# Ranks of the second sort: the last 392 columns of edges ranked in layer 0 instead of beside the sorting network

## The reference, cut to what matters

```python
x = _layernorm(x + L0(x, edges))             # mean of x[src] by dst, two matmuls, rows normalized
x = _layernorm(x + L1(x, weight, types))     # relation matrices, (x @ W_r)[src] * w summed by dst
x = _layernorm(x + L2(x, edges))             # 5 rounds: m = h @ W; agg = segment_sum(m[src], dst); GRU
x = _layernorm(x + L3(x, edges, edge_attr))  # edge MLP on x[src], x[dst], attr, summed by src
```

## Time and profile before

| | us |
|---|---|
| median of 3 runs | 9063.8 (9062.63 to 9071.94) |
| profiled execution, its own time | 9073.26 |
| its span, first to last instruction | 9071.5 |
| POOL busy | 6524.4 (72%) |
| PE busy | 6295.3 (69%) |
| DVE busy | 5542.8 (61%) |
| ACT busy | 2574.8 (28%) |

### The profile page before, as it was taken

The page is one execution under the profiler, slowest core; times in us unless marked ns, Lnnn a source line. Parts: engine busy times, 40 slices in busy tenths (PEclk is TensorE's granted clock), DMA queues, the critical chain, the costliest instruction groups (busy, mean ns, idle before and its releaser), DMA issues. The chain is left out here.

```text
span 9071.5 us, 161491 instructions
## 1 busy us (share of the span) xinstructions
PE 6295.3 (69%) x36545; PEld 5409.3 (60%) x36546; DVE 5542.8 (61%) x13908; ACT 2574.8 (28%) x6581; POOL 6524.4 (72%) x7005
## 2 busy tenths in 40 slices
PE   0011255552444498888888888888888999889998
PEld 0000133332333377777777677767776888778887
DVE  9999444442444466656665566656664666556666
ACT  4223111112333211121112111111112333456665
POOL 1777777777777777767777677767776777657776
PEclk9755566665555599999999999999999999989999
DMA  4000222222222244434443444444443444212223
GB/s 153 7 7 18 58 79 77 78 68 61 59 59 59 80 143 137 138 103 143 137 138 108 137 139 136 129 117 138 138 138 104 135 124 127 71 53 63 64 64 53
DMA packets 428100, 870.71 MB, mean 96 GB/s; under 512 B 117433, under 2 KB 229680, under 8 KB 427349
## 3 DMA queue, kind: packets, MB, share of 16 engines
q0 software_dynamic: 269952, 615.62, 25.2%
q10 hardware_dynamic: 122250, 189.76, 6.2%
q1 hardware_dynamic: 35529, 61.49, 2.1%
HBM read 763.02 MB, written 103.40 MB: 96 GB/s over the span
## 5 line engine op out<-in xcount | busy, mean ns | idle before, releaser
L1027 POOL DMA_INDIRECT rows<-state_table,rec x3440 | 3290.6, 957 | 1185.9 <-issue 1105.8
L1100 PE MATMUL l_prod<-rows,onehot 128*125 x10728 | 2640.3, 399 | 1210.6 <-SPq L1041 523.8
L1141 DVE TENSOR_TENSOR agg<-agg,l_prod 125x256 f32 (+2 forms) x5364 | 2038.7, 380 | 2185.2 <-PE l_prod L1100 1156.2
L1100 PEld LDWEIGHTS l_prod<-rows,onehot 128*125 128x125 f32 x10728 | 2010.8, 223 | 1637.4 <-issue 1440.4
L2313 POOL DMA_INDIRECT w_area<-xcol_table,l_slots x832 | 787.7, 947 | 346.6 <-issue 250.4
L1027 POOL DMA_INDIRECT rows<-rel_table,rec x782 | 740.4, 947 | 255.5 <-issue 238.2
L1027 POOL DMA_INDIRECT rows<-in_x_dram,rec x782 | 740.8, 947 | 251.2 <-issue 232.0
L1837 PE MATMUL l_prod<-l_sources,rec 125*125 125x256 f32 x3000 | 695.1, 382 | 24.6 <-DMA rec<-dense_table 23.9
L474 POOL DMA_INDIRECT slots_table<-rec_stage,row_stage x528 | 553.1, 1048 | 161.6 <-issue 143.2
L1837 PEld LDWEIGHTS l_prod<-l_sources,rec 125*125 125x125 f32 x3000 | 562.9, 189 | 118.2 <-DMA rec<-dense_table 30.8
L1792 PE MATMUL l_rh<-state,w_area 128*128 x4000 | 591.0, 282 | 3.0 <-DVE l_u L2121 3.0
(11 more groups left out here) (427 smaller groups left out, 10314.1 us busy)
## 6 DMA issues: line engine op xcount, KB each, us to landing
rec<-dense_table ACTq DMA_DIRECT2D x125, 732.4 KB
rows<-state_table,rec POOLq DMA_INDIRECT x3440
l_sources<-state_table ACTq DMA_DIRECT2D x125, 250.0 KB
rel_table<-l_relrow ACTq DMA_DIRECT2D x50, 500.0 KB
state_table<-l_row ACTq DMA_DIRECT2D x200, 125.0 KB
dense_table<-late_rec SPq DMA_DIRECT2D x50, 366.2 KB
w_area<-xcol_table,l_slots POOLq DMA_INDIRECT x832
rows<-in_x_dram,rec POOLq DMA_INDIRECT x782, 2.5
```

The lines of the kernel that those rows point to most:

```text
L1027: pool.indirect_dma_start(out=K["rows"][:, r, 0:width], out_offset=None, in_=table, in_offset=bass.IndirectOffsetOnAxis(ap=K["rec"][:, wor ...
L1100: last = pe.matmul(slots[k][0:LANES, 0:width], K["onehot"][:, h % ONEHOTS, k, :], rows[:, bass.ds(at[k], width)], start=True, stop=True)
L1141: dve.tensor_tensor(into, into, of, ALU.add).then_inc(S.added, 1)
```

## The change

Of the 784 columns now 392 are late (four of the eight parts), and so POOL scatters 392 in the sort and not 528. Only the first four parts (40 rank turns) are ranked in the sort. POOL keeps the tile numbers, the spare rows and the running bases of the other four in SBUF (`late_bucket`, `late_row`, `late_base`). DVE makes their 40 rank turns in layer 0: five behind every second gather turn, eight times, from turn 4 on; the hardware loop of turns 3 to 24 becomes eight loops of two turns and one of six. All operands of these rank turns lie in SBUF (the numbers compared with, the scan's result and the copies' data too). Their row addresses go to a DRAM table of their own, and a late load is two DMAs. ACT packs the late records in two passes of 196 columns, at turns 16 and 18 of the network. Late columns: 16 in layer 1, 63 in each of rounds 0 to 3, and 124 behind the last round's gathers, in two batches of 62; the second is loaded after SP's relay of the last round and after the first batch has landed.

```diff
-LATE_PIECES = 7
+LATE_PIECES, LATE_PASSES = 6, 2
-LATE = 256
-LATE_LAYER0, LATE_LAYER1, LATE_ROUND, LATE_LAST = 0, 10, 46, 62
+LATE = 392
+LATE_LAYER1, LATE_ROUND, LATE_LAST = 16, 63, 62
+RANK_TILES = 5
+RANK_TURNS = TILES // RANK_TILES
@@ sort_edges, SP
-            sp.wait_ge(late_made, LATE_PIECES)
-            sp.dma_start(T["late"], late_all[:].rearrange("p c w -> p (c w)")).then_inc(late_out, 16)
+            for n in range(LATE_PASSES):
+                sp.wait_ge(late_made, (n + 1) * LATE_PIECES)
+                sp.dma_start(T["late"][:, n * AT_ONCE * REC2:(n + 1) * AT_ONCE * REC2],
+                             late_area[:, 0:AT_ONCE * REC2]).then_inc(late_out, 16)
@@ sort_edges, POOL
+            pool.tensor_copy(K["late_bucket"], bucket[:, NOW:C]).then_inc(late_kept, 1)
+            pool.tensor_copy(K["late_row"], spare[:, NOW:C]).then_inc(late_kept, 1)
+            pool.tensor_copy(K["late_base"], base[:]).then_inc(late_kept, 1)
@@ sort_edges, ACT
-                    if rows and turn == LAST_TURN - 1:
-                        put_late(6 - (k.bit_length() - 1))
+                    if rows and turn in (LAST_TURN - 3, LAST_TURN - 1) and k > 1:
+                        put_late((turn - LAST_TURN + 3) // 2, 7 - k.bit_length())
@@ sort_edges, DVE
-                    turns_now = min(ranked + RANKS_A_TURN, PARTS * TILES // FIVE)
+                    turns_now = min(ranked + RANKS_A_TURN, NOW // PART * TILES // FIVE)
@@ layer0, DVE
+            def rank_turn(turn):
+                ...
+                dve.tensor_copy(is_tile[:, :, 0], K["late_base"][:, tiles])
+                step(dve.tensor_tensor(is_tile[:, :, 1:PART + 1], bucket[:, None, :].to_broadcast(part),
+                                       K["iota_row"][:, tiles][:, :, None].to_broadcast(part), ALU.is_equal))
+                step(dve.tensor_tensor_scan(rank..., carry..., is_tile..., 0.0, ALU.mult, ALU.add))
+                dve.tensor_copy(K["late_base"][:, tiles], rank[:, :, PART])
+                for n in range(RANK_TILES):
+                    ...
+                    dve.copy_predicated(other_row if place % 2 else row, is_tile[:, n, 1:PART + 1].bitcast(I32),
+                                        rank[:, n, 1:PART + 1]).then_inc(row_set, 1)
+                ...
-            turns(dve, 0, body)
+            for i in range(3):
+                body(Turn(dve, 0, i))
+            pieces = LATE_PARTS * 2
+            for piece in range(pieces):
+                with dve.Fori(3 + 2 * piece, 5 + 2 * piece) as i:
+                    body(Turn(dve, 0, i))
+                for turn in range(piece * RANK_TURNS // 2, (piece + 1) * RANK_TURNS // 2):
+                    rank_turn(turn)
+            with dve.Fori(3 + 2 * pieces, TURNS - 1) as i:
+                body(Turn(dve, 0, i))
@@ Late
+        sp.dma_start(self.K["late_rows"][:, 0:n], self.T["late_rows"][:, self.read:self.read + n])\
+            .then_inc(self.loaded, 16)
@@ layer2, SP and POOL
             relay_rows(nc, sp, K, S, LAST, NEAR, NEAR_VISITS)
+            late.load(sp, LATE_LAST)
...
+            late.scatter(pool, LATE_LAST, 2 + rounds)
```

More of the change, by code:

```diff
@@ L1507, in _, with scratch @@
             dve.sem_inc(S.added, CREDIT)
-            dve.wait_ge(loaded, 16 * 12)
-            turns(dve, 0, body)
+            def scratch(at, n):
+                return K["code_block"][:, at:at + n]
+            many = RANK_TILES * (PART + 1)
+            is_tile, rank, carry = (a.rearrange("p (n c) -> p n c", n=RANK_TILES)
+                                    for a in (scratch(0, many), scratch(many, many), K["late_carry"]))
+            other_row, slot_f, low_f = (scratch(2 * many + k * PART, PART) for k in range(3))
@@ new lines, in _ @@
+            slot_i, low_i = (scratch(2 * many + k * PART, PART).bitcast(I32) for k in range(3, 5))
+            def rank_turn(turn):
+                q, t = divmod(turn, RANK_TURNS)
+                step = Steps(dve, rank_step, 2 + q * (RANK_TURNS * 2 + 7) + t * 2 + (1 if t > 0 else 0))
+                row, bucket = (K[n][:, q * PART:(q + 1) * PART] for n in ("late_row", "late_bucket"))
+                part = [SLOT, RANK_TILES, PART]
+                tiles = slice(t * RANK_TILES, (t + 1) * RANK_TILES)
+                if t == 0:
+                    step(dve.memset(other_row, 0.0))
+                dve.tensor_copy(is_tile[:, :, 0], K["late_base"][:, tiles])
+                step(dve.tensor_tensor(is_tile[:, :, 1:PART + 1], bucket[:, None, :].to_broadcast(part),
+                                       K["iota_row"][:, tiles][:, :, None].to_broadcast(part), ALU.is_equal))
+                step(dve.tensor_tensor_scan(rank.rearrange("p n c -> p (n c)"), carry.rearrange("p n c -> p (n c)"),
+                                            is_tile.rearrange("p n c -> p (n c)"), 0.0, ALU.mult, ALU.add))
+                dve.tensor_copy(K["late_base"][:, tiles], rank[:, :, PART])
+                for n in range(RANK_TILES):
+                    place = turn * RANK_TILES + n
+                    if place > 1:
+                        dve.wait_ge(row_set, place - 1)
+                    dve.copy_predicated(other_row if place % 2 else row, is_tile[:, n, 1:PART + 1].bitcast(I32),
+                                        rank[:, n, 1:PART + 1]).then_inc(row_set, 1)
+                dve.wait_ge(row_set, (turn + 1) * RANK_TILES)
+                if t == RANK_TURNS - 1:
+                    step(dve.tensor_tensor(row, row, other_row, ALU.add))
+                    step(dve.tensor_copy(low_i, row))
+                    step(dve.tensor_scalar(slot_i, low_i, 7, None, ALU.arith_shift_right))
+                    step(dve.tensor_scalar(low_i, low_i, SLOT - 1, None, ALU.bitwise_and))
+                    dve.tensor_copy(slot_f, slot_i)
+                    step(dve.tensor_copy(low_f, low_i))
+                    step(dve.scalar_tensor_tensor(bucket.bitcast(I32), low_f, float(PITCH), slot_f, ALU.mult, ALU.add))
+                    dve.sem_inc(rows_done, 1)
@@ L1512 @@
+            with dve.Fori(3 + 2 * pieces, TURNS - 1) as i:
+                body(Turn(dve, 0, i))
+            for i in range(TURNS - 1, TURNS + 1):
+                body(Turn(dve, 0, i))
 class GatedWeights:
@@ L2511, in gnn @@
         K["far_key"] = K["w_area"][:, 4 * BLOCKS:4 * BLOCKS + FAR]
+        at = 4 * BLOCKS + FAR
+        for name, n in (("late_bucket", LATE), ("late_row", LATE), ("late_base", TILES),
+                        ("late_carry", RANK_TILES * (PART + 1))):
+            K[name] = K["w_area"][:, at:at + n]
+            at += n
         K["code_block"], K["weight_block"] = (K["w_area"][:, k * 2 * BLOCKS:(k + 1) * 2 * BLOCKS] for k in range(2))
```

60 lines of the change are left out of this document (36 added, 24 removed).

## The result

The changed kernel takes 9082.83 us (median of 9 runs, 9080.11 to 9102.17) where the kernel before took 9062.39 us (median of 9, 9053.83 to 9071.94). The ratio is 1.0027, with a 95% interval of 1.0017 to 1.0037: it is slower by 0.27%, which is 24 us by the ratio and 20.4 us by the medians, where I had forecast 9059 us and no measurable change. The profiled execution took 9102.17 us, with a span of 9100.4 us, 28.9 us more than before's span of 9071.5.

A forecast was written before the change was run, and what follows sets the result against it. No engine was taken to bound the kernel throughout; each stage had its own limit. Terms -153 + 137 + 7.6 + 1 + 2.5 = -5 us took the median from 9063.8 to 9059 us, range 9030 to 9092.

The forecast's parts named there:

- Sort (-153): Sort and barrier: DVE ends at 831.2 us, layer 0 starts at 834 instead of 987.7; -153 us (-147 to -156).
- The step's lowest, 2.8 us: Barrier behind the sort: between 2.8 and 8.95 us, taken as 3 because DVE is now last.
- Layer 0 (+137): Layer 0: the added DVE rank turns count in full on the PE, DVE, ACT chain; +137 us (131 to 147).
- Rival A: Layer 0: the chain catches up behind rank-turn blocks; 9013 us if a third is absorbed, 8922 if all; chance 0.25.
- rival B: Layer 0: POOL's DMAs lock DVE out, 0.7 to 2.5 us per rank turn, giving 9088 to 9159 us; chance 0.13.
- step 2: Sort, POOL: 392 of 528 scatters end at 780 us, 50 us before DVE, covering the three new copies.
- Steps 4 to 7: Layer 0 through last round: +137, +7.6, +1 and +2.5 us, with a scatter costing 1.266 us.
- layer 1 (+15.4 for 7.6): Layer 1, ended by POOL: six more scatters at 1.266 us cost +7.6 us (6 to 8).
- rounds 0 to 3 (+28.8 for 1): Rounds 0 to 3: 17 more scatters, 21.5 us, nearly fit POOL's waits for the stores; +1 us (0 to 6).
- rival C: Rounds and end: late scatters and stores delay each other by 5 us a round, giving 9084 us; chance 0.1.
- Step 7: Last round: POOL done at 7983.9, plus 8.95 us behind its last scatter, gives 7992.9; +2.5 us (0 to 8).
- The 5.3 us between the two batches: Last round: the first batch's landing, about 1.3 us, and the load, 3.7, with issue take 5.3 us.

The follow-up runs named there:

- e1: Changed kernel with the 40 rank turns taken out of layer 0, its loops still split: 8957.98 us, ratio 0.9890.
- e8: Changed kernel with its three copies at the sort's end made by ACT in place of POOL: 9058.25 us, ratio 0.9985.
- f1: Changed kernel with those copies on ACT and the 40 rank turns moved from layer 0 to layer 1, one at a time: 8943.77 us, ratio 0.9862.
- e2: Kernel before with three POOL copies (392, 392, 50 columns) behind the sort's last scatter, results unread: 9100.95 us beside 9061.77.
- e5: Kernel before with one POOL copy of 392 columns and its wait behind the sort's last scatter: 9116.59 us beside 9072.33.
- e6: Kernel before with three POOL copies of 8 columns each behind the sort's last scatter: 9102.15 us beside 9072.33.
- e10: Kernel before with one POOL copy of 392 columns as the sort's last instruction, without semaphore or wait: 9108.64 us beside 9068.69.
- e12: Kernel before with a 392-column POOL copy, then a 50-column memset, ending the sort; slow chip, far scatters 971 ns against 962 in the sort.
- e13: Kernel before with a 128-column POOL copy as layer 0's first POOL instruction; slow chip, far scatters 967 ns against 958 in the sort.
- e14: Kernel before with a 128-column POOL copy right ahead of layer 0's first gather; slow chip, far scatters 971 ns against 962 in the sort.
- e17: Kernel before with a 128-column POOL copy right ahead of layer 0's first gather, run beside an unchanged control; slow chip, 14 us below the control.
- e15: Kernel before with 128-column POOL copies ahead of layer 0's first gather and ahead of its far scatters; slow chip, layer 1's gathers 955 ns.
- e16: Kernel before, unchanged, traced as a control on a slow chip, where the kernel before took 11,759.59 to 11,775.03 us.

## Why the prediction was wrong

**Sort (-153): right.** DVE ended at 830.97 + 0.24 = 831.21 us, forecast 831.2, and layer 0's first instruction came 1.2 us behind it, where I took 3. The step's lowest, 2.8 us, was thus too long, and it gives -154: the -156 in the range had no term behind it.

**Layer 0 (+137): right in kind, 5 us too high.** Two scans of a block are 3.09 us apart, forecast 3.04. So 40 x 3.09 and the 11 us of address steps and memsets make 135 us; measured are 130.8 (`e1`). The loops' starts and restarts of the chain, which I had put at 6 us, don't show: `e1` has the split loops and is 1.1 us over the kernel before. The waits in layer 0 from its first gather to its last, of PE in the kernel before, then of PE and POOL in the changed one:

```profile
PE l_prod L1100 <- DVE agg L1141: 200.7, 98, 5.6
PE l_trs L1311 <- DVE l_x L1198: 188.6, 46, 5.0
```

```profile
PE l_trs L1328 <- DVE l_x L1211: 317.4, 46, 21.9
PE l_prod L1113 <- DVE agg L1154: 198.9, 97, 3.6
...
POOL rows L1040 <- SPq L1059: 134.4, 29, 19.1
```

The wait for the additions didn't grow. 129 us lie in the wait for the normalised row of DVE that a block of rank turns delays, up to 21.9 us at a time, and POOL waits for ring places as forecast. Rival A (absorption) and rival B (DVE locked out) are refuted by the same numbers; in B rank turns would be 3.7 to 5.5 us long. That POOL was the one to wait, as that part's row suggested, is seen beside these scans:

```profile
1154.07 1.19 DVE L1546 TENSOR_TENSOR_SCAN w_area<-w_area 128x495 f32<-128x495 f32 x1
...
1154.52 1.50 POOL L1040 DMA_INDIRECT rows<-in_x_dram,rec  x1 [0.30 <-issue]
```

This gather, started inside the scan, takes 1.50 us; the one before it took 0.95. The other order, a scan that starts inside a gather:

```profile
1241.80 1.40 POOL L1040 DMA_INDIRECT rows<-in_x_dram,rec  x1 [0.30 <-issue]
...
1242.41 1.19 DVE L1546 TENSOR_TENSOR_SCAN w_area<-w_area 128x495 f32<-128x495 f32 x1
```

Here the gather had been running for 0.61 us, and it is again the gather that is stretched, to 1.40 us, while the scan takes its 1.19. The Trainium skill, "SBUF — State Buffer", section "Who interferes with whom", lets issue order decide who waits. The first pair agrees with that. The second doesn't, and the measurement decides: in both orders it is POOL that waits, and the 40 scans of layer 0 take 1.19 us in the median and 1.23 at most, so rival B didn't come.

**The step that failed: in step 2, "the three new copies (below 2 us each) are covered".** Their own time was indeed covered: POOL then sat idle for 58 us. What I never asked is whether they change the price of what POOL does later. Steps 4 to 7 take 1.266 us a scatter and an unchanged gather from the kernel before, and the edge MLP has no term at all; 6324 DMAs stand behind the sort. Without the copies on POOL (`e8`) the sum of the stages is -12.7 us against my -5, and the ratio 0.9985 would have been within what I called no change. With them, layer 1 (+15.4 for 7.6), rounds 0 to 3 (+28.8 for 1) and the edge MLP (+7.2 for 0) are over by 42.8 us; `e8` gives 33.6 of that back. In the table's sum the layer 0 term, 5 us too high, hides some of it.

**What is left, in `e8`.** Layer 1 is +8.6, forecast 7.6. Rounds 0 to 3 are +8.3, forecast 1 with 6 as its upper end: at two of the boundaries POOL waits 3.4 and 4.2 us behind its 63 scatters, while in `f1` all four gaps are 0.3 us and the rounds +1.2. That would fit rival C, stores and scatters that delay each other, but no run tests it, and it stays open. The last round is -4.1, forecast +2.5. Step 7 put 8.95 us between POOL's last scatter and SP's first load of the edge MLP. In `e8` that scatter ends at 7972.97 + 0.96 = 7973.93 and the load is issued 2.7 us later, so this term was 6 us too high:

```profile
7972.97 0.96 POOL L1095 DMA_INDIRECT slots_table<-late_rec,late_rows  x1 [0.30 <-issue]
...
7976.65 0.80 SPq L2343 DMA_DIRECT2D l_slots<-slots_table  x2
```

The 5.3 us between the two batches had no row for the 1.3 us of a scatter's landing in it; the whole wait measured 5.6 us in the changed kernel and 6.4 in `e8`.

**Range and chances.** 9082.83 lies inside 9030 to 9092, but this is luck: what made the kernel slower, a dearer DMA, was in none of the cases that I had named. C gives nearly the same time, 9084, for another reason. The kernel got slower, clear of the noise, where I had given 0.48 to no change and 0.22 to slower.

## What to carry to other kernels

An instruction moved to an idle engine isn't free because it is short: compare the duration of the engine's other instructions before and after, in medians by line, before explaining a miss by the schedule; the sort's gain of 155 us and layer 0's loss of some 130 left little, and 8 ns on 4400 serial DMAs, 35 us, turned it into a loss. In a program like this one, keep plain copies off POOL between its last scatter and its first gather, or give them to an idle ACT. And work that costs its full time in a stage paced by a chain (130 us) can cost a tenth in a stage paced by DMAs (11 us), if it comes in small pieces: the waits for landed rows in the profile say which stage that is, and how much fits.

## What the runs showed of the hardware that I had not expected

- POOL's indirect DMAs have two levels that differ by 8 to 9 ns of some 950, and in these traces a program keeps the one that its first gather has. One POOL copy of 128 or 392 columns, or three of 8 to 392, between the last scatter and the first gather put it on the dear one in all ten programs that had it (the changed kernel, `e1`, `e2`, `e5`, `e6`, `e10`, `e12`, `e13`, `e14` with its repetition `e17`, and `e15`), at 30 to 44 us over the kernel before in the four single runs where nothing else was changed and the chip was not a slow one (`e2`, `e5`, `e6`, `e10`). What lies behind it is open: no run separates a gather from other kinds of DMA as the one that fixes the level.
- Separate from this, the same code reads 958 or 962 ns for the sort's scatters in different executions: the kernel before 962 in its first profile and 958 in `e16`; on one chip, `e5` 962 and `e6` 958, whose sorts are the same up to there.
- A DVE scan of 495 elements can stretch one of POOL's gathers whether it starts before or after it (1.50 and 1.40 us for 0.95), and keeps its own 1.19 us.
- On two chips the kernel before took 11,759.59 to 11,775.03 us for 9062 to 9072 elsewhere, though DVE's additions are 380 ns in both and PE's matmuls of L1100 only 4% longer (417 ns for 399, at a mean granted clock of 0.81 for 0.84). What grew most is idle time. I didn't look into the cause.

```profile
L1141 DVE TENSOR_TENSOR agg<-agg,l_prod 125x256 f32 (+2 forms) x5364 | 2039.2, 380 | 3405.9 <-remote 1011.5 <-issue 932.6 <-PE l_prod L1100 799.6
```

This row is `e16`'s; in the kernel before it reads 380 ns as well, with 2185.2 us of idle time.
